# Recommender head on one core: inner rows in two stacked and two full tiles, gram copies split over SyncE and GpSimd, loads bound to other gathers

## The chip, the cores and the metric

The kernel runs on 1 core of one Trainium2 chip. The metric is the device time of one execution in microseconds (us). Three runs of the kernel before have a median of 208.22 us (207.81 to 209.19).

## The reference, cut to what matters

```python
sparse_embed = emb_tables[field_idx[None, :], x_sparse]        # 512 samples x 26 fields x 64, float32
z = sparse_embed.reshape(B, 26 * 64)                           # 1664 columns
gram = einsum('bik,bjk->bij', sparse_embed, sparse_embed)
inner = gram[:, iu, ju]                                        # 325 pairs i < j
dnn_in = concatenate([x_dense, z, inner], axis=-1)             # 13 + 1664 + 325 = 2002 columns
h = relu(dnn_in @ w1 + b1)                                     # w1 is 2002 x 2002
out = sigmoid(h @ w2 + b2)                                     # 512 x 1
```

## The kernel before, in words

**The product.** The 512 samples are four batch tiles of 128 (bt 0 to 3). The 2002 rows of w1 and the row of b1 lie in 16 tiles (K tiles t0 to t15) of up to 128 rows: t0 to t12 hold z (two tiles for a group of four fields, t12 alone for the last two fields), and t13 to t15, the inner tiles, hold the 325 pairs, the 13 dense columns and a row of ones for b1, with 117, 123 and 111 rows. The 2002 columns are cut into two halves (h 0, h 1) of two chunks of 500 or 502. A float32 product is made of three fp32r products: each operand is split into hi (its fp32r rounding, a cast on ScalarE) and lo (the rest, a subtraction on VectorE), and TensorE runs hi*hi, x_hi*w_lo and x_lo*w_hi. So one `product` (one w piece t, h with one bt) is 3 terms x 2 chunks = 6 matmuls of about 500 columns (L1071 to L1073 where it is the last of its sum, L1081, L1084 and L1087 elsewhere), and all of it is 16 x 2 x 4 = 128 products, 768 matmuls.

**The w pieces.** SyncE loads each piece of 500 KB into one of 5 buffers `w_raw` (L778), ScalarE casts it to `w_hi` (L849), VectorE makes `w_lo` in two halves (L931); there are 7 buffers for each of these. Phase A uses a piece for bt 0 and 1 (32 pieces), phases B1 (h 1) and B2 (h 0) for bt 2 and 3 (another 32). A load waits for the `w_lo` of the piece five before it, and up to load 26 also for a given number of gathers (`GATE`). The 1 MB of w2 goes behind load 28 (L781).

**The embeddings.** GpSimd issues 104 gathers (L823), each 128 rows of 256 bytes, four to one *arrival* (one bt, one group of four fields; two for the last group). Gathers 0 to 51 are for bt 0 and 1, gathers 52 to 103 for bt 2 and 3. From gather 52 on a short memset `pace` (L834) stands behind each. Gathers 56 and 60 are held until gram rounds 2 and 4 are done (`HELD_BACK`). VectorE transposes an arrival (L948, L944 for the last group), ScalarE casts it to `x_hi` (L875), VectorE makes `x_lo` (L961), and both copy it into `ET`, the layout of the gram matmuls.

**The gram rounds.** 64 small matmuls each (L1041): four rounds for bt 0 and 1, four for bt 2 and 3 together. Both engines copy the result from PSUM into `G` (L893, L979), and then DMAs put it into `x_in`, the rows of the inner tiles: pairs of a field below 13 with one of 13 or above go straight from G (*cross* pairs, L792, three DMAs for a bt), the pairs within one half of the fields go to `gram_dram` in HBM (*store*, L797, two DMAs) and from there skewed into `x_in` (*fetch*, L804, two DMAs of 84 rows, some of which carry pairs twice against rows of zeros in w). All seven are on SyncE's queue, in order with the w loads.

**The order.** `make_todo` writes TensorE's order by hand; `make_orders` plays the engines against each other with a table of durations (`PE_LEN`, `LAND` and so on), may pull a step of TensorE's forward where the next is not ready, and from that come the four lists that ScalarE, VectorE, TensorE and SyncE run strictly in order. GpSimd's order is the loop over the arrivals. TensorE starts with 25 matmuls on ones, and puts two more of 512 columns (`KEEP`, L1020) before its fourth product. Phase A ends with the inner tiles of bt 0 and 1, phase B with those of bt 2 and 3, after which only the last drains and the sigmoid are left.

## Time and profile before

| | us |
|---|---|
| median of 3 runs | 208.22 (207.81 to 209.19) |
| the profiled execution | 207.65 |
| its span | 205.1 |
| TensorE busy in it | 197.8 (96%) |
| VectorE, ScalarE, GpSimd busy | 146.6, 129.6, 118.5 |
| bytes moved | 38.99 MB, 190 GB/s on the mean |

The span is what the instructions cover; 2.55 us of the execution lie outside it. Times of rows are us from the start of the span. A busy time is what an engine spends in instructions; of a matmul the end is modelled, so that neighbouring rows overlap a little, and the distance from start to start is the better measure.

### The profile page before, as it was taken

The numbers are of one execution on the slowest core, as the hardware profiler recorded it, in microseconds if no ns is written. First come the engines' busy times: TensorE is split into PE (matmuls) and PEld (weight loads), VectorE is DVE, ScalarE is ACT, GpSimd is POOL, SyncE is SP. The second block draws the span as 40 slices with busy tenths as digits, with TensorE's granted clock in tenths as the row PEclk, the third lists the DMA queues.
The fourth block names the chain that finished last, engine by engine and source line by source line (L and its number), as shares of the span: only waits on it lengthen the run. The fifth ranks groups of instructions, "written<-read, shape, count | busy, mean of one in ns | idle before, by whom it ended". The sixth has DMA issues, their size and how long they took to land.

```text
span 205.1 us, 3837 instructions
## 1 busy us (share of the span) xinstructions
PE 197.8 (96%) x1334; PEld 160.8 (78%) x1334; DVE 146.6 (71%) x343; ACT 129.6 (63%) x260; POOL 118.5 (58%) x162
## 2 busy tenths in 40 slices
PE   8979999999999999989998999999999999999994
PEld 8946788888888778767885888888888887788882
DVE  3566877777885898679449999492978687563473
ACT  2766644778964999487528755676899946542201
POOL 4778778777777787369888988898920000000000
PEclk9999999999999999999999999999999999999998
DMA  5689767777776069837937748778598186023000
GB/s 153 179 254 312 234 220 225 216 231 207 225 231 250 20 208 316 297 71 209 370 124 224 209 140 268 276 249 298 132 327 280 13 283 210 6 48 59 28 0 0
DMA packets 15387, 38.99 MB, mean 190 GB/s; under 512 B 3881, under 2 KB 5281, under 8 KB 15369
## 3 DMA queue, kind: packets, MB, share of 16 engines
q1 hardware_dynamic: 11688, 35.27, 51.7%
q0 software_dynamic: 3328, 3.41, 8.6%
q8 instruction: 10, 0.16, 0.3%
q10 hardware_dynamic: 353, 0.08, 0.2%
q14 instruction: 8, 0.07, 0.1%
HBM read 37.71 MB, written 0.69 MB: 187 GB/s over the span
## 4 chain that ended last, share of the span: by engine, by line
PE 74%; DMA 8%; POOL 7%; DVE 4%; issue 3%; ACT 1%; DVEq 0%; ACTq 0%; POOLq 0%
PE slot L1081 23%; PE slot L1084 22%; PE slot L1087 22%; DMA E<-emb,row_idx 7%; POOL E L823 7%; PE slot L1041 3%; DVE slot L1005 1%; PE slot L1073 1%; PE slot L1071 1%; PE slot L1072 1%; DVE w_lo L931 1%; DMA x_idx<-idx 1%; PE slot L1020 1%; POOL pace L834 1%; DVE G L979 1%
## 5 line engine op out<-in xcount | busy, mean ns | idle before, releaser
L823 POOL DMA_INDIRECT E<-emb,row_idx x104 | 108.8, 1046 | 31.2 <-issue 23.7
L931 DVE TENSOR_TENSOR w_lo<-w_raw,w_hi 128x500 fp32r<-128x500 f32 (+6 forms) x128 | 80.6, 670 | 9.4 <-ACT w_hi L849 9.0
L849 ACT CAST w_hi<-w_raw 128x1000 fp32r<-128x1000 f32 (+6 forms) x64 | 65.0, 1028 | 22.7 <-DMA w_raw<-w 18.8
L1081 PE MATMUL slot<-w_hi,x_hi 128*128 128x500 f32 (+5 forms) x236 | 74.7, 397 | 1.4 <-ACT x_hi L867 1.0
L1084 PE MATMUL slot<-w_lo,x_hi 128*128 128x500 f32 (+5 forms) x236 | 73.4, 391 | 1.6 <-DVE w_lo L931 1.5
L1087 PE MATMUL slot<-w_hi,x_lo 128*128 128x500 f32 (+5 forms) x236 | 72.7, 389 | 0.0
L1084 PEld LDWEIGHTS slot<-w_lo,x_hi 128*128 128x128 f32 (+2 forms) x236 | 44.5, 188 | 11.8 <-DVE w_lo L931 2.7
L1081 PEld LDWEIGHTS slot<-w_hi,x_hi 128*128 128x128 f32 (+2 forms) x236 | 43.3, 189 | 12.5 <-ACT x_hi L875 1.7
L1087 PEld LDWEIGHTS slot<-w_hi,x_lo 128*128 128x128 f32 (+2 forms) x236 | 44.5, 189 | 9.1
L880 ACT COPY ET<-T 32x128 f32<-32x128 f32 (+4 forms) x86 | 31.1, 362 | 2.0
L948 DVE STREAM_TRANSPOSE T<-E 128x256 f32<-128x256 f32 x24 | 10.6, 441 | 19.3 <-DMA E<-emb,row_idx 19.2
L875 ACT CAST x_hi<-T 128x256 fp32r<-128x256 f32 x24 | 9.7, 406 | 14.5 <-DVE T L948 14.1
L966 DVE COPY ET<-T 32x128 f32<-32x128 f32 (+3 forms) x58 | 15.1, 261 | 1.8
L893 ACT COPY G<-slot 26x208 f32<-26x208 f32 x34 | 11.0, 324 | 7.5 <-PE slot L1041 6.7
L979 DVE COPY G<-slot 26x208 f32<-26x208 f32 x30 | 11.1, 370 | 4.2 <-PE slot L1041 3.4
L1005 DVE SCALAR_TENSOR_TENSOR slot<-slot,w_all 128x500 f32<-128x500 f32 (+1 forms) x16 | 10.7, 696 | 2.1 <-PE slot L1073 2.0
L1041 PEld LDWEIGHTS slot<-ET 64*64 64x64 f32 x512 | 8.7, 135 | 3.1 <-issue 2.4
L961 DVE TENSOR_TENSOR x_lo<-x_in,x_hi 117x128 fp32r<-117x128 f32 (+2 forms) x12 | 3.5, 292 | 10.5 <-ACT x_hi L867 10.5
L867 ACT CAST x_hi<-x_in 117x128 fp32r<-117x128 f32 (+2 forms) x12 | 3.6, 297 | 11.8 <-DMA x_in<-G 6.3
L961 DVE TENSOR_TENSOR x_lo<-T,x_hi 128x256 fp32r<-128x256 f32 x24 | 10.0, 418 | 1.3 <-ACT x_hi L875 1.2
L1041 PE MATMUL slot<-ET 64*64 64x52 f32 x512 | 9.7, 221 | 0.2 <-DVE G L979 0.2
L1013 PE MATMUL slot<-ones 128*128 128x128 f32 x50 | 8.3, 345 | 1.0 <-POOL ones L813 1.0
(39 smaller groups left out, 81.3 us busy)
## 6 DMA issues: line engine op xcount, KB each, us to landing
w_raw<-w SPq DMA_DIRECT2D x32, 501.0 KB, 4.7
w_raw<-w SPq DMA_DIRECT2D x32, 500.0 KB, 4.3
E<-emb,row_idx POOLq DMA_INDIRECT x104, 4.0
w_all<-w SPq DMA_DIRECT2D x1, 1001.0 KB
gram_dram<-G SPq DMA_DIRECT2D x8, 84.5 KB
x_in<-gram_dram SPq DMA_DIRECT2D x8, 42.0 KB
x_in<-G SPq DMA_DIRECT2D x4, 58.5 KB
x_in<-G SPq DMA_DIRECT2D x4, 19.5 KB
```

The lines of the kernel that those rows point to most:

```text
L823: nc.gpsimd.indirect_dma_start(out=E[:, k % ER, j, :], out_offset=None, in_=emb_rows, in_offset=bass.IndirectOffsetOnAxis(ap=row_idx[:, at ...
L849: nc.scalar.copy(w_parts(m)[0], w_source(m)).then_inc(w_hi_ready, 1)
L880: nc.scalar.copy(*et_copy(bt, part, i, h, half)).then_inc(et_by_act, 1)
L931: nc.vector.tensor_tensor(lo[:, cols], w_source(m)[:, cols], hi[:, cols].bitcast(F32), ALU.subtract)\
L961: nc.vector.tensor_tensor(lo, src, hi.bitcast(F32), ALU.subtract).then_inc(x_split, 1)
L966: nc.vector.tensor_copy(*et_copy(bt, part, i, h, half)).then_inc(et_by_dve, 1)
L979: nc.vector.tensor_copy(gram_place(bt % 2, s, rnd), gram_view(bt, s, b)).then_inc(g_copied_dve, 1)
L1005: nc.vector.scalar_tensor_tensor(out=acc, in0=acc, scalar=0.0, in1=w2_all[:, at:at + width], op0=ALU.max, op1=ALU.mult, accum_out=parts[:, ...
L1041: last = nc.tensor.matmul(slot[AUX[bt]][64 * c:64 * c + 64, at:at + 2 * FIELDS], e.rearrange("k s f -> k (s f)"), e[:, :, 0:FIELDS], start ...
L1081: nc.tensor.matmul(acc[q], xh, hi[:, cols[q]], start=first, stop=False)
L1084: nc.tensor.matmul(acc[q], xh, lo[:, cols[q]], start=False, stop=False)
L1087: last = nc.tensor.matmul(acc[q], xl, hi[:, cols[q]], start=False, stop=False)
```

## The change

**The inner rows.** They are now 339 rows (each pair once, dense, ones) in four tiles. 85 of them (`BOTH`: 78 cross pairs and 7 dense) are in the tiles TERMS_A (t13) and TERMS_B (t14), which hold the three terms as rows of one matmul: in TERMS_A rows 0 to 84 of `x_hi` meet `w_lo`, in TERMS_B rows 0 to 84 of `x_lo` (written into `x_hi` by VectorE) meet `w_hi`, and rows 85 and up of both carry hi*hi, 42 and 43 of them. The other 254 rows are in FULL_0 (t15) and FULL_1 (t16), with three matmuls a chunk as before. So a half of one bt takes 1 + 1 + 3 + 3 = 8 passes for its inner rows where it took 9. There are 68 w pieces for 64, and 4 casts of `x_in` a bt for 3.

**The copies.** SyncE makes four cross DMAs for a bt. GpSimd makes the two stores and now four fetches (36, 42, 42, 36 rows), at fixed places among the gathers (`BY_POOL`: the store of bt 0 before gather 58, its fetch before 60, the store of bt 1 before 61, its fetch before 63; those of bt 2 and 3 behind the last gather). SyncE no longer waits for a store.

**Loads and order.** Loads 2 to 9 and 26 wait for other gathers, w2 goes ahead of load 26 behind gather 47, `KEEP` is 1 for 2, the dense rows are loaded by SyncE in three DMAs. In phase B the B1 products of the last group (t10, t11) come after three groups of B2 instead of four, and the gram rounds of bt 2 and 3 stand among other B2 products.

```diff
-CROSS = [(0, 9), (9, 12), (12, 13)]
-IT = len(CROSS)
+IT = 4
 NT = ZT + IT
-CROSS_AT = [0, 0, DENSE]
-WITHIN_ROWS, WITHIN_COLS = HALF - 1, (HALF + 1) // 2
-WITHIN = WITHIN_ROWS * WITHIN_COLS
-WITHIN_AT = {1: 3 * HALF, 2: DENSE + HALF}
-ONES_AT = WITHIN_AT[2] + WITHIN
-KROWS = [P] * ZT + [9 * HALF, WITHIN_AT[1] + WITHIN, ONES_AT + 1]
+TERMS_A, TERMS_B, FULL_0, FULL_1 = range(ZT, NT)
+BOTH = 6 * HALF + 7
+CROSS_AT = [(TERMS_A, 0, 0, 6), (TERMS_A, BOTH + 3, 0, 3), (TERMS_B, BOTH + 4, 3, 6), (FULL_0, 0, 6, HALF)]
+SHORT = 6
+LONG = SHORT + 1
+WITHIN_AT = [(FULL_0, 7 * HALF, 0, SHORT, 2 * SHORT, SHORT), (FULL_1, 7, 0, 0, SHORT, LONG),
+             (FULL_1, 7 + SHORT * LONG, 1, 0, SHORT, LONG),
+             (FULL_1, 7 + 2 * SHORT * LONG, 1, SHORT, 2 * SHORT, SHORT)]
+KROWS = [P] * ZT + [BOTH + 3 + 3 * HALF, BOTH + 4 + 3 * HALF, 7 * HALF + SHORT * SHORT,
+                    7 + 2 * SHORT * LONG + SHORT * SHORT]
+DENSE_AT = [(TERMS_A, 6 * HALF, list(range(7)) + [0, 1, 2]), (TERMS_B, BOTH, [3, 4, 5, 6]),
+            (FULL_1, 1, [7, 8, 9, 10, 11, 12])]
+ONES_ROW = (FULL_1, 0)
 INNER_TILES = list(range(ZT, NT))
 IN_KEY = GROUPS_Z
+KEY_A, KEY_B = IN_KEY, IN_KEY + 1
+LO_AT = {t: n for n, t in enumerate(t for t in range(NT) if t not in (TERMS_A, TERMS_B))}
...
-GATE = {3: 4, 4: 5, 5: 7, 6: 8, 7: 9, 8: 11, 9: 12, 10: 15, 11: 16, 12: 19, 13: 20, 14: 23, 15: 24, 16: 27, 17: 28,
-        18: 31, 19: 32, 20: 35, 21: 36, 22: 39, 23: 40, 24: 41, 25: 43, 26: 51}
-CONSTS_BEHIND = 28
-KEEP_AT, KEEP = 3, 2
+GATE = {2: 3, 3: 3, 4: 6, 5: 7, 6: 8, 7: 11, 8: 12, 9: 13, 10: 15, 11: 16, 12: 19, 13: 20, 14: 23, 15: 24, 16: 27, 17: 28,
+        18: 31, 19: 32, 20: 35, 21: 36, 22: 39, 23: 40, 24: 41, 25: 43, 26: 50}
...
+CONSTS_AHEAD, CONSTS_GATE = 26, 47
+KEEP_AT, KEEP = 3, 1
...
+PACED_FROM = 3
 UNPACED = 52
+BY_POOL = {58: [("store", 0)], 60: [("fetch", 0)], 61: [("store", 1)], 63: [("fetch", 1)],
+           N_GATHERS: [("store", 2), ("store", 3), ("fetch", 2), ("fetch", 3)]}
...
         todo += b_group("B1", 1, g)
-        todo += b_group("B2", 0, GROUP_ORDER[n]) if n < 4 else []
-    rest = [s for g in GROUP_ORDER[4:] for s in b_group("B2", 0, g)]
-    todo += mixed(rest[:7], gram({2, 3}), every=2) + rest[7:]
+        todo += b_group("B2", 0, GROUP_ORDER[n]) if n < 3 else []
+    rest = [s for g in GROUP_ORDER[3:] for s in b_group("B2", 0, g)]
+    todo += rest[:1] + mixed(rest[1:9], gram({2, 3}), every=2) + rest[9:]
     later = [inner("B1", 1, 2), inner("B1", 1, 3), inner("B2", 0, 2), inner("B2", 0, 3)]
-    todo += [s for steps in later for s in steps[:1]] + [s for steps in later for s in steps[1:]]
+    todo += [s for steps in later for s in steps[:2]] + [s for steps in later for s in steps[2:]]
...
+def shelf(pieces, m):
+
+    return m - sum(PIECES[n][1] == TERMS_B for n in pieces[:m + 1])
+
+
+def earlier(pieces, m):
+
+    return [n for k, n in enumerate(pieces[:m]) if shelf(pieces, k) == shelf(pieces, m) - HL]
...
+        def cross_moves(bt):
+
+            rows = Q * (bt % 2)
+            return [(t - ZT, x_in[at:at + HALF * (b - a), bt, t - ZT, :], G[rows + a:rows + b, HALF:FIELDS, :])
+                    for t, at, a, b in CROSS_AT]
+
+        def within_store(bt, u):
+
+            within, rows = slice(HALF * u, HALF * (u + 1)), Q * (bt % 2) + HALF * u
+            return gram_dram[bt, u].rearrange("(i j) b -> i j b", i=HALF), G[rows:rows + HALF, within, :]
+
+        def within_fetches(bt):
+
+            skewed = [gram_dram[bt, u, 0:2 * SHORT * (HALF + 1), :].rearrange("(a e) b -> a e b", e=HALF + 1) for u in (0, 1)]
+            return [(t - ZT, x_in[at:at + (b - a) * far, bt, t - ZT, :], skewed[u][a:b, 1:far + 1, :])
+                    for t, at, u, a, b, far in WITHIN_AT]
...
-                    if m == EARLY:
-                        sp.wait_ge(e_landed[0], 16 * GROUP_GATHERS[LAST])
+                    if m == CONSTS_AHEAD:
+                        sp.wait_ge(paced, paced_count(CONSTS_GATE))
+                        sp.dma_start(w2_all[:], w2.rearrange("n o -> (o n)").partition_broadcast(P))\
+                          .then_inc(consts_landed, 16)
+                        sp.dma_start(b2_all[:], b2.partition_broadcast(P)).then_inc(consts_landed, 16)
                     if m in GATE:
-                        sp.wait_ge(paced, GATE[m] - SOON + 1)
-                    if m >= RAW:
-                        sp.wait_ge(w_split, 2 * (m - RAW + 1))
+                        sp.wait_ge(paced, paced_count(GATE[m]))
+                    if m >= RAW and PIECES[USED[m - RAW]][1] == TERMS_B:
+                        sp.wait_ge(w_hi_ready, w_hi_count(m - RAW))
+                    elif m >= RAW:
+                        sp.wait_ge(w_split, w_split_count(m - RAW, 1))
 
                     sp.dma_start(w_raw[:, m % RAW, 0:HALF_W[h]], w1[t, :, HALF_AT[h]:HALF_AT[h] + HALF_W[h]])\
                       .then_inc(w_landed[m % RAW], 16)
...
-                if op == ("load", CONSTS_BEHIND):
-                    sp.dma_start(w2_all[:], w2.rearrange("n o -> (o n)").partition_broadcast(P))\
-                      .then_inc(consts_landed, 16)
-                    sp.dma_start(b2_all[:], b2.partition_broadcast(P)).then_inc(consts_landed, 16)
-                if op[0] == "store":
+                if op == ("load", EARLY + 1):
+                    sp.wait_ge(pads_ready, 2)
...
+                        at += len(cols)
+                if op[0] == "cross":
                     bt = op[1]
-                    rows = Q * (bt % 2)
                     sp.wait_ge(g_copied_act, evac_count("act", rounds_of(bt)))
                     sp.wait_ge(g_copied_dve, evac_count("dve", rounds_of(bt)))
-                    if bt == 0:
...
+                    for m, to, src in cross_moves(bt):
+                        sp.dma_start(to, src).then_inc(cross_landed[bt][m], 16)
...
+            def move(part, bt):
+                if part == "store":
+                    pool.wait_ge(g_copied_act, evac_count("act", rounds_of(bt)))
+                    pool.wait_ge(g_copied_dve, evac_count("dve", rounds_of(bt)))
+                    for u in (0, 1):
+                        pool.dma_start(*within_store(bt, u)).then_inc(g_stored[bt], 16)
+                if part == "fetch":
+                    pool.wait_ge(g_stored[bt], 32)
+                    for m, to, src in within_fetches(bt):
+                        pool.dma_start(to, src).then_inc(within_landed[bt][m], 16)
+
...
             at = 0
             for k, (bt, g) in enumerate(ARRIVALS):
+                for part in BY_POOL.get(at, []):
+                    move(*part)
...
                 for j in range(GROUP_GATHERS[g]):
+                    for part in BY_POOL.get(at, []) if j else []:
+                        move(*part)
                     nc.gpsimd.indirect_dma_start(
...
+                    if g == KEY_B:
+                        dve.wait_ge(x_hi_ready, x_hi_count(bt, KEY_A))
+                        b = slice(bt * P, (bt + 1) * P)
+                        nc.vector.tensor_tensor(x_hi[0:BOTH, TERMS_B, b], x_in[0:BOTH, bt, TERMS_A - ZT, :],
+                                                x_hi[0:BOTH, TERMS_A, b].bitcast(F32), ALU.subtract).then_inc(x_split, 1)
+                    else:
...
+                    if t in (TERMS_A, TERMS_B):
+
+                        if t == TERMS_A:
+                            pe.wait_ge(x_hi_ready, x_hi_count(*key_of(step)))
+                        else:
+                            pe.wait_ge(x_split, x_lo_count(*key_of(step)))
+                            pe.wait_ge(w_hi_ready, w_hi_count(RANK[n]))
+                        for q in (0, 1):
+                            if t == TERMS_A:
+                                pe.wait_ge(w_split, w_split_count(RANK[n], q))
+                            last = nc.tensor.matmul(acc[q], xh, hi[:, cols[q]], start=first, stop=end)
+                            if end and q == 0:
+                                last.then_inc(half_done, 1)
```

What this moves is seen at two places. The first is where bt 0's gram is copied out, at the end of phase A. On SyncE's queue before (`x_in<-G` is a cross DMA, `gram_dram<-G` a store, `x_in<-gram_dram` a fetch, `w_raw` a load; the two bt follow each other):

```order
L778 DMA w_raw<-w 128x1000 x2
L792 DMA x_in<-G 117x1x128
L797 DMA gram_dram<-G 13x1664 x2
L792 DMA x_in<-G 39x1x128
L792 DMA x_in<-G 13x1x128
L804 DMA x_in<-gram_dram 84x1x128 x2
L778 DMA w_raw<-w 128x1000
```

SyncE's queue now, at the same place:

```order
L861 DMA w_raw<-w 128x1000
L875 DMA x_in<-G 78x1x128
L875 DMA x_in<-G 39x1x128 x2
L875 DMA x_in<-G 91x1x128
L861 DMA w_raw<-w 128x1000 x3
```

And GpSimd's now, where before only `DMA E` and `MEMSET pace` alternate; the first `DMA E` here is gather 57, the one behind the first fetches is gather 60:

```order
L908 DMA E<-emb,row_idx 128x64
L919 MEMSET pace 128x64
L891 DMA gram_dram<-G 13x1664 x2
L908 DMA E<-emb,row_idx 128x64
L919 MEMSET pace 128x64
L908 DMA E<-emb,row_idx 128x64
L919 MEMSET pace 128x64
L895 DMA x_in<-gram_dram 36x1x128
L895 DMA x_in<-gram_dram 42x1x128 x2
L895 DMA x_in<-gram_dram 36x1x128
L908 DMA E<-emb,row_idx 128x64
L919 MEMSET pace 128x64
```

Twelve DMAs (these six and the same six for bt 1) are now issued between gathers 57 and 63, and each gather from 58 on stands behind some or all of them.

The second place is TensorE's last product of bt 1's z and the first inner products of bt 0 (slot1 is the sum of bt 1, slot0 that of bt 0). Before, from the last rows of t11 over t13 to the first of the next product:

```order
L1087 MATMUL slot1<-w_hi,x_lo 128x500
L1081 MATMUL slot0<-w_hi,x_hi 128x502
L1081 MATMUL slot0<-w_hi,x_hi 128x500
L1084 MATMUL slot0<-w_lo,x_hi 128x502
L1084 MATMUL slot0<-w_lo,x_hi 128x500
L1087 MATMUL slot0<-w_hi,x_lo 128x502
L1087 MATMUL slot0<-w_hi,x_lo 128x500
L1081 MATMUL slot0<-w_hi,x_hi 128x502
```

Now, with TERMS_A and TERMS_B (L1176, two matmuls each; the lo buffer of a shared shelf holds the w of TERMS_B), and then FULL_0:

```order
L1202 MATMUL slot1<-w_hi,x_lo 128x500
L1176 MATMUL slot0<-w_hi,x_hi 128x502
L1176 MATMUL slot0<-w_hi,x_hi 128x500
L1176 MATMUL slot0<-w_lo,x_hi 128x502
L1176 MATMUL slot0<-w_lo,x_hi 128x500
L1196 MATMUL slot0<-w_hi,x_hi 128x502
L1196 MATMUL slot0<-w_hi,x_hi 128x500
L1199 MATMUL slot0<-w_lo,x_hi 128x502
```

The first tile that needs a fetch (t14 before, FULL_0 now) comes after 4 matmuls instead of 6.

## Rows read from the trace of the kernel before

**Rows 1.** The page: span, busy times, and TensorE's granted clock in 40 slices.
```profile
span 205.1 us, 3837 instructions
PE 197.8 (96%) x1334; PEld 160.8 (78%) x1334; DVE 146.6 (71%) x343; ACT 129.6 (63%) x260; POOL 118.5 (58%) x162
...
PEclk9999999999999999999999999999999999999998
```

**Rows 2.** Waits of TensorE: waited for, us in total, times, longest.
```profile
PE slot L1084 <- DVE w_lo L931: 1.5, 2, 1.0
...
PE slot L1081 <- ACT x_hi L867: 1.0, 1, 1.0
```

**Rows 3.** Timeline of TensorE, phase B: start, us, instruction, xcount, [idle before].
```profile
160.93 0.62 PE L1081 MATMUL slot<-w_hi,x_hi 128*128 128x500 f32 x2
...
162.29 0.61 PE L1081 MATMUL slot<-w_hi,x_hi 128*128 128x500 f32 x2
...
166.48 1.18 PE L1041 MATMUL slot<-ET 64*64 64x52 f32 x64
...
201.69 0.39 PE L1073 MATMUL slot<-w_hi,x_lo 111*128 111x500 f32 x1
```

**Rows 4.** Timeline of all engines, the start of phase A.
```profile
7.29 0.95 POOL L823 DMA_INDIRECT E<-emb,row_idx  x1 [0.30 <-issue]
11.34 0.31 DVE L944 STREAM_TRANSPOSE T<-E 128x128 f32<-128x128 f32 x1 [1.39 <-DMA E<-emb,row_idx]
```

**Rows 5.** Timeline where bt 1's fourth group arrives, at the end of phase A.
```profile
71.14 0.41 ACT L875 CAST x_hi<-T 128x256 fp32r<-128x256 f32 x1
71.60 0.71 PE L1081 MATMUL slot<-w_hi,x_hi 128*128 128x500 f32 x2
```

**Rows 6.** Timeline of SyncE and GpSimd around the copies of bt 0 and 1.
```profile
80.47 0.95 POOL L823 DMA_INDIRECT E<-emb,row_idx  x1 [0.16 <-issue]
...
81.08 1.00 SPq L792 DMA_DIRECT2D x_in<-G  x1
...
82.13 1.01 SPq L797 DMA_DIRECT2D gram_dram<-G  x2
...
87.51 2.43 SPq L804 DMA_DIRECT2D x_in<-gram_dram  x2
...
88.83 0.95 POOL L823 DMA_INDIRECT E<-emb,row_idx  x1 [4.68 <-DVE T L948]
...
90.64 0.84 SPq L792 DMA_DIRECT2D x_in<-G  x1
91.53 1.25 SPq L797 DMA_DIRECT2D gram_dram<-G  x2
...
92.91 1.29 POOL L823 DMA_INDIRECT E<-emb,row_idx  x1 [0.16 <-issue]
...
95.63 1.62 SPq L804 DMA_DIRECT2D x_in<-gram_dram  x2
```

**Rows 7.** Gathers: by form over the span, the last, its arrival, and landings from 94 to 151.
```profile
L823 POOL DMA_INDIRECT E<-emb,row_idx x104 | 108.8, 1046 | 31.2 <-issue 23.7 <-DVE T L948 4.8 <-DVE row_idx L918 1.8
...
148.92 1.18 POOL L823 DMA_INDIRECT E<-emb,row_idx  x1 [0.16 <-issue]
...
153.67 0.45 DVE L948 STREAM_TRANSPOSE T<-E 128x256 f32<-128x256 f32 x1 [0.58 <-DMA E<-emb,row_idx]
...
E<-emb,row_idx POOLq DMA_INDIRECT x41, 3.7
```

**Rows 8.** SyncE: stores and fetches by tile: count: ns min/median/max, first to last.
```profile
L797 SPq DMA_DIRECT2D gram_dram<-G x8: 453/505/693, 82.1 to 185.7; - x8
L804 SPq DMA_DIRECT2D x_in<-gram_dram x8: 756/786/1597, 87.5 to 190.5; - x8
```

**Rows 9.** Waits on the fetched rows in the last stage of phase B.
```profile
188.00 3.22 SPq L804 DMA_DIRECT2D x_in<-gram_dram  x4
190.31 0.30 ACT L867 CAST x_hi<-x_in 123x128 fp32r<-123x128 f32 x1 [2.35 <-DMA x_in<-gram_dram]
```

214 lines of the change are left out of this document (118 added, 96 removed).

## The prediction

> **What bounds the kernel now.** I read the page first: TensorE is busy 197.8 of 205.1 us [rows 1], so time is won by giving it less, or lost by making it wait. Then its waits: 2.5 us in three places in all of phases A and B [rows 2]. Next the timeline of TensorE, for the price of a step: the product that starts at 160.93 ends where the next starts, at 162.29, so 6 matmuls take 1.37 us, one 0.228; the gram round at 166.48 lasts 1.18 and costs some 1.3 with the restart behind it [rows 3]. The last matmul starts at 201.69 and ends at 202.1; the 3.0 us from there to the end of the span are drains, sigmoid and the store, which the change leaves as they are. The profiled execution took 207.65, 0.57 under the median of 208.22, so the sum is made on 202.1 for TensorE's end and its difference is put on the median.
>
> Last I looked for who comes just in time. GpSimd does: its gathers go out back to back until 148.92, and the arrival that ends with that one is turned at 153.67 [rows 7]. TensorE takes it at 160.93 [rows 3].
>
> **What is removed.** Eight passes for nine over the inner rows, 2 chunks, 4 bt, 2 halves: 16 matmuls x 0.228 = 3.65 us less, all of it on TensorE, which waits for little. Four more w pieces cost ScalarE 4 casts, VectorE nothing (TERMS_B has no lo) and the queues 2 MB on 39; with ScalarE busy 129.6 of 205.1 and VectorE's count unchanged [rows 1] they have cover.
>
> **The start.** The fourth gather goes out at 7.29 and its arrival is turned at 11.34 [rows 4], 4.0 us later; load 2 is issued behind the first arrival, in the midst of that. It now waits for this gather, and a filler matmul pair is gone. Up to 1.5 us could be won here. But bt 1's fourth group reaches x_hi at 71.14 + 0.41 = 71.55, and TensorE takes it at 71.60 [rows 5]: 45 us later phase A is at the pace of the gathers, which are not sooner. Whoever is early there waits there. Bounds 0 and 1.5; I take 0.3, near the row that binds.
>
> **The copies of bt 0 and 1, and what stands behind them.** SyncE gets free: its fetch at 87.51 had waited for the store of 82.13 [rows 6] with the loads behind. GpSimd takes that wait. Before, it had a hole from 84.0 to 88.83, held by the gram rounds [rows 6]; that hides a part. Its clock now, with s for a store DMA and f for a fetch DMA: gather 57 at 80.47, next free at 81.75; bt 0's gram has been copied by 81.08, so the two stores go at once. Gathers 58 and 59 take 2 x 1.28. The stores land 4.4 us after they are issued (83.14 to 87.51 [rows 6]), then four fetches. Gather 60 not before 88.83. Store of bt 1 not before 90.6, gathers 61 and 62, landing at most 2.9 (92.78 to 95.63), four fetches, gather 63, which went at 92.91.
>
> The trace has no plain DMA issued by GpSimd, so s and f are bounded from both sides. Below: SyncE's shortest of these, 0.45 [rows 8]. Above: a gather on GpSimd itself, 1.05 on the mean and 1.28 from start to start [rows 6, 7]. I take SyncE's medians for the same shapes, with the gap that GpSimd shows: s 0.55 and f 0.80 (0.50 and 0.79 [rows 8]), since 13 or 40 rows are less to write than a gather's 128. Then: stores to 82.85, gathers to 85.4, landing 87.25, fetches to 90.45, gather 60 to 91.7, stores to 92.8, gathers to 95.4, landing 95.7, fetches to 98.9. Gather 63 is D = 6.0 us late, and so is each of the 40 behind it, as GpSimd has no idle time later in which to catch up. At 0.45 each D is 3.2, at 1.25 it is 12.4.
>
> Against this, DMAs from GpSimd have a rule of their own. The gathers here last 1.05 on the mean against 0.95 for most single ones [rows 6, 7], though VectorE copies ET from SBUF to SBUF between them. The Trainium skill (SBUF — State Buffer, "Who interferes with whom") says that a VectorE copy in its two-port mode shuts GpSimd out, descriptor writing with it, and gives 620 ns alone against 3100 beside such a copy. The trace does not show a gather three times as long, so that end is not used; 0.62 for each of the twelve would, as an estimate from that page, give D of 5.
>
> **What the late gathers cost.** The order now asks sooner: from the product that takes the last arrival (B1, t10, bt 3) to TensorE's end there are 24 full products, 8 short ones of 2 matmuls and 4 gram rounds, 24 x 1.37 + 8 x 0.456 + 4 x 1.33 = 41.8 us, and before there were 26 products and 4 rounds, 40.9 (202.1 - 160.93 is 41.2). The last gather goes at 148.92 + D, lands 3.7 (median of 41) to 4.75 later (its own, 153.67 - 148.92) [rows 7], and transpose 0.45, cast 0.41 and two hand-overs make 0.95 [rows 5, 7]. So TensorE can't end before 148.92 + 4.2 + 0.95 + 41.8 + D = 195.9 + D. With no wait for gathers it would end at 202.1 - 3.65 - 0.3 = 198.15. The first is the later one as soon as D is over 2.3. With D = 6.0 it is 201.9: 0.2 under the 202.1 of before. The 3.95 us won are given back to within 0.2 in waits for x_hi in B1.
>
> **Waits that this covers.** FULL_0 of bt 0 is wanted some 1.0 earlier than t14 was (4 matmuls for 6 ahead of it, and the start), and its fetch is issued at 88.05 against 87.51, FULL_1's last by 90.45. With a landing of 2.3 (188.00 to 190.31 [rows 9]) to 3.3, x_hi is there at 91 to 93 and TensorE waits 1 to 2 us where it waited 1.0 [rows 2], and about 1 again at bt 1. These waits come before the B arrivals, so below some 3.5 in sum they only shorten those. At the end the fetches of bt 3 are issued by some 11 us behind the last copy from PSUM and land at 13.5; FULL_1 of bt 3 is wanted 17.3 behind the last gram round (7 products, 8 short ones, 3 full ones), of which the copies take some 2: nothing. VectorE runs its list in order, and transposes late by D hold the w_lo behind them; I count 0.1 for it, bounds 0 and 1.5.
>
> **Sum.** 207.65 - 0.2 + 0.1 = 207.55, and on the median's scale 208.1.
>
> **Rivals.** *GpSimd's plain DMAs cost nearly what its gathers do (slower).* The place is gathers 58 to 63. For it: GpSimd writes descriptors for a plain copy too, and a good part of a gather's 0.95 [rows 6] may be fixed. Against: a tenth to a third of the rows. At 1.0 each D is 9.4 and TensorE ends at 205.3, the time is 211.4; at 1.25 D is 12.4 and the time 214.4. It decides from D = 8.2, some 0.87 each, where 1% is lost. If waits for x_hi grow to several us the granted clock, full until the last slice before [rows 1], could also drop; no row prices that.
>
> *They are cheap, or arrivals land sooner (faster).* With TensorE waiting, loads thin out, and half of the landings are under 3.7 as it is [rows 7]. At 0.5 each D is 3.5; with a landing of 3.7 the end is 198.9, the time 205.0; nothing under 198.15 less a full start, 196.9. For it: SyncE's rows, and its queue no longer blocks loads. Typical of it is 205.2.
>
> *The start pays in full and carries.* Gathers 56 and on hang on gram rounds, so D moves with TensorE; if the arrivals of phase A land sooner for loads 4 to 9 standing behind other gathers, 1.2 more is won, 206.9. It stays within 1%, and is part of the forecast's case.
>
> *The stacking doesn't shorten anything.* The short matmuls have 127 and 128 rows and the same 500 columns; rows of 111, 117 and 128 rows all take 0.228. Not likely, and it would add 3.65 only if gathers didn't bind.
>
> **How the numbers follow.** Forecast (D of 4.5 to 8, waits in B1 for most of what was won): 0.37, 206.4 to 210.3. Dear DMAs: 0.31. Cheap ones: 0.32. The measurement tells about 1% from no change, so faster by over 1% has 0.32, within 1% 0.37, slower by over 1% 0.31. The range for 8 in 10 leaves a tenth at either side: 204.5 (D near 3.2, part of the start) to 213.3 (1.15 each).
>
> **What would show it.** Right: 752 matmuls of 500 columns, GpSimd's DMA rows at 0.55 to 0.8, gather 63 at 98 to 100 and the last at 154 to 156, and 3 to 5 us of TensorE's waits on x_hi L962 between 110 and 160, the longest at t10. Wrong: gather 63 before 96 with TensorE's end under 200, or after 101; waits in B on w_lo and not on x_hi; more than 4 us of waits at t15 and t16 in phase A; or a granted clock under full in B.

## The result: slower by 1.7%, and the profile after

The changed kernel took 212.43 us (211.73 to 212.49, 4 runs) beside 208.7 us for the kernel before (207.81 to 209.95, 4 runs), a ratio of 1.0166 with a 95% interval of 1.0105 to 1.0228. The profiled execution took 211.73 us with a span of 209.8, before 207.65 with 205.1 [rows 1]. The forecast was no change (208.1): the time lies inside the range, on the slower side. The medians here and below are of all runs, and the ratios leave out the few that fell in a slower state of the chip, the profiled one of i1 among them.

From the page of the changed kernel: span, busy times, TensorE's granted clock in 40 slices, the chain by engine.

```profile
span 209.8 us, 3872 instructions
...
PE 198.1 (94%) x1316; PEld 160.6 (77%) x1316; DVE 147.3 (70%) x345; ACT 135.0 (64%) x267; POOL 133.3 (64%) x186
...
PEclk9997899999999999997999999999996999999999
...
PE 50%; POOL 24%; DMA 12%; issue 5%; DVE 3%; SPq 3%; ACT 2%; ACTq 0%; DVEq 0%; POOLq 0%
```

TensorE has 16 matmuls and a filler less and is busy for as long as before, because the clock row, full before, has three dents. GpSimd holds 24% of the chain that ended last, where its share had been 7%; before, the row was:

```profile
PE 74%; DMA 8%; POOL 7%; DVE 4%; issue 3%; ACT 1%; DVEq 0%; ACTq 0%; POOLq 0%
```

The DMAs that I could only bound are cheap. GpSimd's stores and fetches by tile (ns min/median/max, first to last start), against SyncE's in [rows 8]:

```profile
L895 POOL DMA_DIRECT2D x_in<-gram_dram x16: 569/608/646, 87.9 to 194.3; - x16
L891 POOL DMA_DIRECT2D gram_dram<-G x8: 518/552/572, 83.2 to 185.8; - x8
```

Now TensorE's waits, with the clock behind each. The timeline of TensorE in the changed kernel (start, us, instruction, [idle before <- releaser]):

```profile
18.23 0.79 PE L1196 MATMUL slot<-w_hi,x_hi 128*128 128x500 f32 x2 [1.79 <-ACT x_hi L962]
...
95.93 0.49 PE L1185 MATMUL slot<-w_hi,x_hi 127*128 127x502 f32 x1 [1.78 <-DVE x_lo L1061]
...
107.37 0.50 PE L1185 MATMUL slot<-w_hi,x_hi 127*128 127x502 f32 x1 [1.43 <-DVE x_lo L1061]
...
157.40 0.72 PE L1196 MATMUL slot<-w_hi,x_hi 128*128 128x500 f32 x2 [1.98 <-ACT x_hi L962]
...
164.52 0.61 PE L1196 MATMUL slot<-w_hi,x_hi 128*128 128x500 f32 x2
...
206.41 0.39 PE L1187 MATMUL slot<-w_hi,x_lo 127*128 127x500 f32 x1
```

And its windows (stretch, length, TensorE busy, granted clock, DMA share, GB/s):

```profile
17.00:18.85 1.85, 0.62 (x3) 0.97 0.87 312
18.85:22.10 3.25, 3.25 (x9) 0.50 0.77 232
22.10:24.00 1.90, 1.90 (x10) 0.99 0.85 251
...
97.20:100.60 3.40, 3.40 (x10) 0.50 0.77 235
...
158.60:161.90 3.30, 3.30 (x9) 0.51 0.04 10
```

Three of the four waits are followed by 3.3 us at half clock, the 1.2 GHz level. A matmul takes 0.415 us there (159.01 to 159.43 in the timeline) for 0.228, so a stretch loses some 1.5 us. GpSimd's timeline around the stores and fetches of bt 0 and 1, against [rows 6]:

```profile
80.87 0.95 POOL L908 DMA_INDIRECT E<-emb,row_idx  x1 [2.75 <-PE slot L1142]
...
83.19 1.12 POOL L891 DMA_DIRECT2D gram_dram<-G  x2
...
87.92 2.39 POOL L895 DMA_DIRECT2D x_in<-gram_dram  x4 [0.79 <-DMA gram_dram<-G]
90.65 1.12 POOL L908 DMA_INDIRECT E<-emb,row_idx  x1 [0.34 <-issue]
...
93.03 1.08 POOL L891 DMA_DIRECT2D gram_dram<-G  x2 [1.09 <-DVE G L1080]
...
97.73 2.39 POOL L895 DMA_DIRECT2D x_in<-gram_dram  x4 [0.79 <-DMA gram_dram<-G]
100.42 1.02 POOL L908 DMA_INDIRECT E<-emb,row_idx  x1 [0.30 <-issue]
...
157.52 1.11 POOL L908 DMA_INDIRECT E<-emb,row_idx  x1
```

Gather 63 goes at 100.42 for 92.91, the last one at 157.52 for 148.92. VectorE's timeline says what a late gather does in phase A:

```profile
103.08 0.36 DVE L1061 TENSOR_TENSOR x_lo<-x_in,x_hi 127x128 fp32r<-127x128 f32 x1
106.50 0.45 DVE L1042 STREAM_TRANSPOSE T<-E 128x256 f32<-128x256 f32 x1 [3.05 <-DMA E<-emb,row_idx]
...
107.04 0.28 DVE L1061 TENSOR_TENSOR x_lo<-x_in,x_hi 127x128 fp32r<-127x128 f32 x1
```

The transpose is that of arrival 17, which ends with gather 63. VectorE is held there for 3.05 us, and behind it in the list stands x_lo of FULL_1 of bt 1, for which TensorE waits at 107.37.

TensorE's wait at 157.40 is for the last arrival but one, that of bt 2, and not for the last one. In phase B, VectorE, then ScalarE:

```profile
156.47 0.45 DVE L1042 STREAM_TRANSPOSE T<-E 128x256 f32<-128x256 f32 x1 [2.02 <-DMA E<-emb,row_idx]
160.16 0.45 DVE L1042 STREAM_TRANSPOSE T<-E 128x256 f32<-128x256 f32 x1
...
162.42 0.40 ACT L962 CAST x_hi<-T 128x256 fp32r<-128x256 f32 x1
```

The first transpose is that of bt 2's arrival, whose last gather went at 151.40, 5.1 us earlier; TensorE takes it at 157.40. The last arrival (bt 3) is cast by 162.82, and TensorE, which does the two products of bt 2's arrival and two of B2 first, takes it only at 164.52.

**Where 4.7 us went, by stage.** Times of TensorE in each profiled execution: start of the first gram round, end of the last one of phase A, start of phase B, end of the last matmul; then GpSimd's last gather, and how far TensorE ends behind it. The start of phase B is marked at the third matmul of the product behind the last inner one, some 0.46 us into it; in f3, f5, j1, k2, l1, m2 and m3 one product of phase B (1.37 us) has already been done at that mark. All kernels stand here, as the experiments are read from the same columns (ratios and medians are with each). Each row is one execution.

| kernel | first gram | gram A ends | B starts | end | last gather | end less gather |
|---|---|---|---|---|---|---|
| before | 73.15 | 88.03 | 107.89 | 202.08 | 148.92 | 53.2 |
| changed | 74.46 | 89.80 | 112.04 | 206.80 | 157.52 | 49.3 |
| e1_keep3 | 74.33 | 90.59 | 114.71 | 206.39 | 158.09 | 48.3 |
| e2_sync | 73.97 | 91.08 | 116.53 | 209.99 | 151.90 | 58.1 |
| e3_order_b | 73.77 | 90.33 | 115.69 | 209.19 | 159.39 | 49.8 |
| e4_before_pool | 74.22 | 89.23 | 112.23 | 206.51 | 155.83 | 50.7 |
| g2_chain_cut | 78.83 | 93.88 | 117.97 | 209.96 | 161.13 | 48.8 |
| g1_chain_cut_no_dma | 77.73 | 92.79 | 111.83 | 203.30 | 154.38 | 48.9 |
| f2_inner_land | 73.01 | 89.04 | 115.72 | 206.79 | 157.14 | 49.7 |
| f3_both_land | 73.10 | 89.13 | 115.50 | 206.27 | 156.53 | 49.7 |
| i1_swap | 74.53 | 93.21 | 114.32 | 210.39 | 159.78 | 50.6 |
| f4_told | 72.95 | 89.07 | 110.64 | 207.39 | 155.91 | 51.5 |
| f5_told_order | 73.02 | 88.81 | 111.31 | 205.05 | 156.65 | 48.4 |
| j1_stores_sync | 73.00 | 89.26 | 111.83 | 206.67 | 158.00 | 48.7 |
| k2_fetch65 | 73.57 | 90.11 | 112.35 | 206.07 | 155.66 | 50.4 |
| k5_fetch65_old | 73.49 | 89.59 | 112.97 | 207.13 | 154.37 | 52.8 |
| l1_act_fetch | 73.10 | 90.12 | 113.76 | 204.67 | 151.71 | 53.0 |
| m1_w2_late | 73.40 | 88.49 | 112.07 | 205.94 | 156.54 | 49.4 |
| m2_w2_act | 74.08 | 89.34 | 113.09 | 204.49 | 153.83 | 50.7 |
| m3_w2_31 | 73.03 | 88.17 | 114.90 | 206.02 | 148.39 | 57.6 |

Changed less before: 1.3 us by the first gram round (this execution has the wait at 16.4 and the half clock behind it), 0.5 in the gram stage, 2.4 from there to phase B, 0.6 in phase B. The stacking takes 8 matmuls, 1.8 us, out of each of the last two, so these lose 4.2 and 2.4; 1.3 + 0.5 + 4.2 + 2.4 - 3.65 = 4.7. Of the 4.2, 2.4 are waits (3.4 in three places between 92 and 108, before 0.97 in one) and 1.5 the clock.

### The profile page after: what moved, and what is told of

It is laid out like the page before. It is cut to its first block, busy times and chain, and to the rows that moved or that the text cites. A ratio compares the mean times of both kernels' runs of the same rounds, so it can differ in the third digit from the quotient of the medians.

```text
span 209.8 us, 3872 instructions
## 1 busy us (share of the span) xinstructions
PE 198.1 (94%) x1316; PEld 160.6 (77%) x1316; DVE 147.3 (70%) x345; ACT 135.0 (64%) x267; POOL 133.3 (64%) x186
## 4 chain that ended last, share of the span: by engine, by line
PE 50%; POOL 24%; DMA 12%; issue 5%; DVE 3%; SPq 3%; ACT 2%; ACTq 0%; DVEq 0%; POOLq 0%
POOL E L908 20%; PE slot L1196 14%; PE slot L1199 13%; PE slot L1202 13%; DMA E<-emb,row_idx 8%; PE slot L1142 4%; SPq L875 3%; POOL pace L919 2%; DMA gram_dram<-G 2%; PE slot L1176 2%; DMA x_in<-G 1%; DVE G L1080 1%; PE slot L1187 1%; PE slot L1185 1%; PE slot L1186 1%
## 5 line engine op out<-in xcount | busy, mean ns | idle before, releaser
L1025 DVE TENSOR_TENSOR w_lo<-w_raw,w_hi 128x500 fp32r<-128x500 f32 (+3 forms) x120 | 75.7, 671 | 12.6 <-ACT w_hi L936 12.3
L936 ACT CAST w_hi<-w_raw 128x1000 fp32r<-128x1000 f32 (+3 forms) x64 | 65.2, 1029 | 22.3 <-DMA w_raw<-w 11.0
L1196 PE MATMUL slot<-w_hi,x_hi 128*128 128x500 f32 (+3 forms) x220 | 70.8, 403 | 4.2 <-ACT x_hi L962 3.8
L1199 PE MATMUL slot<-w_lo,x_hi 128*128 128x500 f32 (+3 forms) x220 | 69.3, 396 | 0.1
L1202 PE MATMUL slot<-w_hi,x_lo 128*128 128x500 f32 (+3 forms) x220 | 68.3, 392 | 0.0
L1196 PEld LDWEIGHTS slot<-w_hi,x_hi 128*128 128x128 f32 (+1 forms) x220 | 41.3, 192 | 14.7 <-ACT x_hi L962 5.4
L1199 PEld LDWEIGHTS slot<-w_lo,x_hi 128*128 128x128 f32 (+1 forms) x220 | 42.3, 192 | 9.5 <-DVE w_lo L1025 0.8
L1202 PEld LDWEIGHTS slot<-w_hi,x_lo 128*128 128x128 f32 (+1 forms) x220 | 42.0, 191 | 8.8
L895 POOL DMA_DIRECT2D x_in<-gram_dram x16 | 9.4, 607 | 5.6 <-DMA gram_dram<-G 4.2
L1185 PE MATMUL slot<-w_hi,x_hi 127*128 127x500 f32 (+2 forms) x20 | 8.5, 423 | 3.2 <-DVE x_lo L1061 3.2
```

Of the source, the lines that this page charges most:

```text
L936: nc.scalar.copy(w_parts(m)[0], w_source(m)).then_inc(w_hi_ready, 1)
L1025: nc.vector.tensor_tensor(lo[:, cols], w_source(m)[:, cols], hi[:, cols].bitcast(F32), ALU.subtract)\
L1196: nc.tensor.matmul(acc[q], xh, hi[:, cols[q]], start=first, stop=False)
L1199: nc.tensor.matmul(acc[q], xh, lo[:, cols[q]], start=False, stop=False)
L1202: last = nc.tensor.matmul(acc[q], xl, hi[:, cols[q]], start=False, stop=False)
```

## The experiments

Four theories came up in turn. A: each wait of some 2 us costs as much again by the clock. B: the late gathers bind phase B. C: the fetched rows come late to the inner stage of phase A. D: VectorE's in-order list passes the gathers' lateness on to the inner stage.

**e1_keep3.** `KEEP_AT, KEEP = 3, 1` became `3, 3`.

> Only the filler before the fourth product changes: 3 matmuls of 512 columns for 1, so that TensorE is busy through the 1.8 us in which it waited at 16.4 us. Theory A (a wait of about 2 us is followed by some 3.4 us at a granted clock of 0.50, and that costs another 1.6 us): the clock stays at full at 19 to 22 us, gram round 2 ends some 1.6 us sooner, gathers 56 and on too, and the time is 1.0 to 1.8 us less than that of the changed kernel, 210.6 to 211.4. Theory B (only the late gathers count, the start is levelled out at the pace of the gathers): within 0.5 us of the changed kernel's 212.4.

211.65 us, ratio 1.0132 (1.0051 to 1.0213). The clock stays full at 19 to 22 and the wait shrinks to 0.39, yet the first gram round begins at 74.33: no sooner than the changed kernel's 74.46. The time is in neither theory's range, and the interval overlaps that of the changed kernel; theory A gets nothing certain.

**e2_sync.** SyncE issues the stores behind its first direct copy, and the fetches:

```diff
-BY_POOL = {58: [("store", 0)], 60: [("fetch", 0)], 61: [("store", 1)], 63: [("fetch", 1)],
-           N_GATHERS: [("store", 2), ("store", 3), ("fetch", 2), ("fetch", 3)]}
+BY_POOL = {N_GATHERS: []}
...
                 sp_events.append((at, ("cross", bt)))
+                sp_events.append((at + 4.0, ("fetch", bt)))
```

> The changed kernel with its 8 stores and 16 fetches issued by SyncE, the fetches four entries behind the copies, every other order as it is. Theory B (GpSimd's own DMAs and the waits in front of them, which hold the gathers back by 7.5 to 8.6 us, are the loss): gather 63 is back at 93 to 95, the last one at 150 to 152, no wait at the product of t10 of bt 2, and the time is 3.5 to 5 us less, 207.5 to 209. Theory A: the waits at 16.4 and at FULL_1 of bt 0 and the slow clock behind them stay, only the third wait with its slow stretch goes: 3 to 3.6 us less, about 209. A rival to both (SyncE, held by its waits for the stores, now issues w loads late): waits on w_hi or w_lo at 90 to 110, and less than 1.5 us won.

213.44 us, 1.0188 (1.0110 to 1.0266): both theories miss, and the rival is borne out. The last gather is at 151.90 as expected and the wait at t10 is gone, and nothing is won. SyncE, which has six more DMAs per bt, issues bt 1's fetches at 101.09 instead of 97.73, and the next w piece only behind them, at 104.14. ScalarE stands 3.27 us at the cast of a w piece, with FULL_1's cast behind it in its list, and TensorE waits 3.2 us for what comes of that. SyncE, ScalarE, TensorE:

```profile
101.09 3.00 SPq L883 DMA_DIRECT2D x_in<-gram_dram  x4
...
108.72 1.02 ACT L944 CAST w_hi<-w_raw 128x1000 fp32r<-128x1000 f32 x1 [3.27 <-DMA w_raw<-w]
...
110.32 0.49 PE L1193 MATMUL slot<-w_hi,x_hi 127*128 127x502 f32 x1 [3.18 <-DVE x_lo L1069]
```

**e3_order_b.** Phase B's order as before:

```diff
-        todo += b_group("B2", 0, GROUP_ORDER[n]) if n < 3 else []
-    rest = [s for g in GROUP_ORDER[3:] for s in b_group("B2", 0, g)]
-    todo += rest[:1] + mixed(rest[1:9], gram({2, 3}), every=2) + rest[9:]
+        todo += b_group("B2", 0, GROUP_ORDER[n]) if n < 4 else []
+    rest = [s for g in GROUP_ORDER[4:] for s in b_group("B2", 0, g)]
+    todo += mixed(rest[:7], gram({2, 3}), every=2) + rest[7:]
```

> The changed kernel with the order of phase B as before (B2 of the fourth group too stands ahead of B1's last group), so that the arrivals of t10 and t11 are asked for some 5 us later. Theory A: the wait of 2.0 us at 155.4 and the 1.5 us of slow clock behind it go, 2.5 to 3.5 us less, 209 to 210. Theory B in its strict form (TensorE can't end before the last gather plus the work that stands behind it): 4 products move ahead of the last arrival, so there is as much to win, the two agree here and differ only in the clock row of 157 to 162. If something else holds phase B, nothing is won.

213.51 us, 1.0188 (1.0107 to 1.0269): both theories miss, and nothing is won, as in the last case. The wait at t10 is gone, but phase B starts at 115.69 in an order that is the changed kernel's up to there (which had 112.04), and at the end TensorE waits 0.7 for a gram copy and 1.6 for rows copied straight from G. So the end of phase A can lie 3 to 4 us apart in two profiled executions with the same lists up to there, and a difference of that size in one row of the table shows nothing by itself.

**e4_before_pool.** The kernel before, with its stores and fetches issued by GpSimd ahead of gathers 58, 60, 61, 63 (the changed kernel's `BY_POOL` and `move`, on the shapes of before).

> The kernel before with one part of the change alone: its 8 stores and 8 fetches on GpSimd at the places where the changed kernel has them, all orders of the other engines as before. The gathers behind become 12 DMAs less 4 late: some 5 us at 0.55 to 0.61 each, with the waits for the stores perhaps 6. The last arrival, turned at 153.67 before and asked for at 160.93, is then ready at 159 to 160. Theory A: no wait over 1 us comes in phase B and the clock stays full, the time is within 1 us of before. Theory B: the order before has the slack, so the same, but every us over 7 of lateness costs one. If the lateness is paid in phase A (FULL fetched rows, in-order transposes), 1 to 3 us slower.

211.79 us, 1.0124 (1.0074 to 1.0173): slower than before by itself, which takes the last of the three cases. No stacking, no new start and no slow clock are in it, and it loses 4.3 us by the start of phase B (1.1 of them by the first gram round, ahead of all that was moved). From its timelines, GpSimd, TensorE and VectorE:

```profile
89.44 1.29 POOL L820 DMA_DIRECT2D x_in<-gram_dram  x2 [2.86 <-DMA gram_dram<-G]
...
93.93 0.72 PE L1101 MATMUL slot<-w_hi,x_hi 123*128 123x502 f32 x2 [1.76 <-ACT x_hi L883]
...
106.41 0.45 DVE L966 STREAM_TRANSPOSE T<-E 128x256 f32<-128x256 f32 x1 [6.56 <-DMA E<-emb,row_idx]
...
107.09 0.72 PE L1107 MATMUL slot<-w_hi,x_lo 123*128 123x502 f32 x2 [1.45 <-DVE x_lo L979]
```

GpSimd stands 2.86 us at the landing of the stores, the fetches go 1.9 later than SyncE's [rows 6], and at bt 1 the transpose of arrival 17 stands ahead of x_lo again.

**g2_chain_cut and g1_chain_cut_no_dma.** FULL_0 and FULL_1 of bt 0 and 1 are made from rows put in place at the start, and don't wait for copies or fetches. So in both, those inner rows are not the gram's; in g1 the stores and fetches of bt 0 and 1 are also left out.

```diff
+                    for t, row in ((FULL_0, 0), (FULL_1, 7)):
+                        sp.dma_start(x_in[row:127, 2:4, t - ZT, :], w1[t, row:127, 0:2 * P]...)
...
-                        for landed, count in arrivals_of(bt, m):
+                        for landed, count in arrivals_of(bt, m) if bt >= 2 or m < 2 else []:
...
+            from_bt = bt + 2 if bt < 2 and m >= 2 else bt
```

> The changed kernel, in which the two tiles FULL_0 and FULL_1 of bt 0 and bt 1 are made from rows that a DMA put in place at the start, and no longer wait for the copies and fetches (so these inner rows are not those of the gram; all stores, copies and fetches are still issued where they were, and the gathers are as late). Theory C (what costs is the wait of the inner stage of phase A for its fetched rows, 3.4 to 5.2 us between 88 and 112 in the four kernels that have the rows fetched late, and what the clock loses behind it): no wait over 0.5 us there, phase B starts at 107.5 to 109 instead of 112 to 115.7; then the late gathers (last one at 156 to 158) bind, TensorE ends no sooner than 157 + 4.2 + 0.95 + 41.8 = 204, and the time is 209.5 to 210.5. Theory B (the gathers alone count): the same time. Theory A (waits wherever they are, with a slow clock behind each): the wait at t10 grows by what is won here, 3 to 5 us in B, and the time stays at 211 to 212.5.

> As the kernel with the chain cut, and the stores and fetches of bt 0 and 1 are left out altogether, so that GpSimd's gathers are on time (gather 63 at 92 to 94, the last one at 149 to 151). Neither the wait for fetched rows nor the late gathers are left: what remains against before is the stacking, 3.65 us less, and the start. Theories B and C alike: 204 to 206 us. If it is over 207, something that is neither of the two costs as much as the stacking wins, and the casts and copies on ScalarE and VectorE or the start are next. The difference to the kernel with the chain cut alone is the price of the 12 DMAs on GpSimd with fetched rows out of the way: 4 to 5 us by theory B, below 2 if the gathers had slack.

g2: 215.83 us, 1.0331 (1.0255 to 1.0408). g1: 208.28 us, 0.9986 (0.9944 to 1.0028). The rows put in place are two DMAs on SyncE ahead of a w piece: both kernels wait some 3 us for w_hi at 21 to 24 (2.7 and 3.0), and g1's first gram round is 3.3 us behind the changed kernel's, g2's 4.4. So the times aren't to be read by themselves, but the stages are. From the first gram round to the end, before takes 128.9 us, the changed kernel 132.3, g2 131.1 and g1 125.6. With neither in the way the changed kernel wins 3.4 us, near the stacking's 3.65, though before had a wait of 0.97 for fetched rows in that stretch that g1 has not; with the 12 DMAs of bt 0 and 1 put back on GpSimd (the only edit between the two) all of it is gone, though no inner tile waits for a fetched row. The medians differ by 7.5 us the same way, where the first gram rounds lie 1.1 apart. g2's forecast of no wait over 0.5 us is missed (2.4 and 1.45 are left), g1's of 204 to 206 by about its late start. That speaks for theory D: in g2 VectorE still stands at the transpose of arrival 17 with x_lo behind it, and TensorE with it. VectorE, then TensorE:

```profile
110.90 0.45 DVE L1046 STREAM_TRANSPOSE T<-E 128x256 f32<-128x256 f32 x1 [2.50 <-DMA E<-emb,row_idx]
...
111.78 0.68 PE L1189 MATMUL slot<-w_hi,x_hi 127*128 127x502 f32 x1 [2.40 <-DVE x_lo L1065]
```

**f2_inner_land and f3_both_land.** The planner's landing times, in f3 also the order of phase A's end:

```diff
-INNER_LAND = (3.9, 4.7, 9.2, 10.4)
+INNER_LAND = (3.9, 4.7, 11.0, 12.5)
...
-    todo += inner_0[2:] + later[0] + [s for steps in later[1:] for s in steps[:2]]
-    todo += [s for steps in later[1:] for s in steps[2:]]
+    todo += later[0][:2] + inner_0[2:] + later[0][2:] + [s for steps in later[1:] for s in steps[:2]]
+    todo += [product("B1", ZT - 1, 1, 2)] + [s for steps in later[1:] for s in steps[2:]]
```

> The changed kernel with the planner told that FULL_0 and FULL_1 come 11.0 and 12.5 us behind the last copy (it assumed 9.2 and 10.4; the trace shows 12.7 from the copies' DMA to the cast of FULL_1 of bt 1). ScalarE and VectorE then do other work ahead of those casts, so that less stands blocked behind them, and TensorE takes the short products first. If in-order blocking (a turn, a w_lo or a cast standing behind one that waits for fetched rows) is a good part of the loss: 0.5 to 1.5 us less than the changed kernel. If the fetched rows themselves are late, within 0.5 us of it.

> The changed kernel with the same numbers for the planner and another order of phase A's end: the short products of both halves ahead of FULL_0 and FULL_1 of bt 0 (0.9 us more for their rows), and the first product of phase B (t12 of bt 2, whose row tile has long arrived) ahead of the FULL products of bt 1, with all short ones (1.4 to 1.8 us more). Theory C: the waits of the inner stage shrink from 3.4 to 5.2 us to 1 to 2.5, phase B's rest starts 2 us sooner, the time is 1 to 2.5 us less than the changed kernel's, 210 to 211.4. Theory B: nothing is won, since the late gathers bind at t10: 212 to 212.5.

f2: 211.79 us, 1.0159 (1.0089 to 1.0230); f3: 213.21 us, 1.0252 (1.0192 to 1.0312). f2 is 0.6 us under the changed kernel with an interval that overlaps its own, f3 missed both ranges. The waits of the inner stage were 6.3 and 5.5 us. In f3 the transpose of arrival 17 waits 5.27 us. Both kernels end 49.7 us behind the last gather, as the changed one does (49.3).

**i1_swap.** One entry of VectorE's list:

```diff
+DVE_OPS.remove(("turn", 17))
+DVE_OPS.insert(DVE_OPS.index(("x_lo", 1, IN_KEY + IT - 1)) + 1, ("turn", 17))
```

> The changed kernel with one entry of VectorE's list moved: the transpose of arrival 17, whose last gather is gather 63 (behind all stores and fetches of bt 0 and 1), stands behind the two subtractions for x_lo of bt 1's last inner tiles instead of ahead of the last one. Theory D (the wait in phase A at 107 to 111 us is that of VectorE, which is held at this transpose for 3 to 5 us with x_lo of FULL_1 behind it): TensorE's wait on x_lo at 107 to 111 (1.4, 2.3, 1.4, 3.2 us in the four kernels with this order) is under 0.6, the time is 1 to 2.5 us less than the changed kernel, 210 to 211.4. Theory C (the fetched rows themselves are late): the wait stays, now on x_hi, within 0.5 us of 212.4. If what is won is paid at t10 in phase B for the late gathers (theory B), the wait moves there and the time stays.

213.11 us, 1.0174 (1.0092 to 1.0256). The wait on x_lo at 109.65 is 0.58, as theory D said; the wait at t10 is 2.69 in place of 1.98, as the last sentence said. D is right about the wait and wrong about the time. The profiled execution is the slowest of the four, 215.17 us, and had lost 3.3 us more than the changed kernel's in the gram stage, ahead of this place, so its wait is worth more here than its stage times.

**f4_told, f5_told_order, j1_stores_sync.** The planner is told what GpSimd's DMAs take (f5: with f3's edits, j1: and the stores on SyncE behind its first copy):

```diff
+MOVES_TAKE = {58: 1.1, 60: 2.9, 61: 1.2, 63: 2.8}
...
                 n = len(g_issued)
+                pool_at += MOVES_TAKE.get(n, 0.0)
```

> The changed kernel with the planner told how long GpSimd is held by its stores and fetches (1.1, 2.9, 1.2 and 2.8 us ahead of gathers 58, 60, 61 and 63; it counted them at nothing), so that it places all transposes, and what hangs on them, by gathers that are 8 us late. The transpose of arrival 17 then stands 10 entries behind x_lo of FULL_1, and t10's products of phase B come 3 products later. Theory D with theory B (late gathers cost only where a list expects them on time): neither the wait at 107 nor the one at 157, the time is 3 to 4.5 us less than the changed kernel, 208 to 209.4. Theory C: the inner stage's waits for fetched rows stay at 2 to 3 us, 210 to 211.

> As the kernel with the planner told of GpSimd's DMAs, and also told that fetched rows come at 11.0 and 12.5 us, with the short products first and t12 of bt 2 ahead of the FULL products of bt 1. Theory D: the last waits of the inner stage go too, 0.5 to 1.5 us less than with the planner told alone, 207 to 208.5. If the order of phase A's end brought nothing in the kernel with that order because it has other costs (a drain, a w piece more in the buffers), it is no faster than with the planner told alone.

> As the one before, with the 8 stores issued by SyncE behind the first of its direct copies (the fetches stay on GpSimd): GpSimd is freed of 4 store DMAs at 0.55 and of its wait for the last copies (1.1 us), so gather 63 goes 2.5 to 3.5 us sooner, at 97 to 98, and the last one at 153.5 to 155. Theory B: another 1 to 3 us less where the late gathers bind, 205.5 to 207.5. If the gathers are no longer what binds: within 0.7 us of the kernel before this one.

212.10 us, 1.0157 (1.0079 to 1.0234); 212.04, 1.0184 (1.0110 to 1.0259); 211.25, 1.0102 (1.0038 to 1.0166). All three forecasts of a gain are missed; f5 is no faster than f4, as its second case had it. Told, the planner has phase B start at 110.64 for 112.04, and TensorE still ends at 207.39, 51.5 behind the last gather: it waits 1.5 us for x_hi at 152.75 and 1.8 for gram copies at 170.91, where two gram rounds now stand one behind the other. In j1 GpSimd has 4 DMAs less before gather 63 and sends it no sooner, at 101.27, for it stands at its fetches until SyncE's stores have landed:

```profile
88.22 2.37 POOL L899 DMA_DIRECT2D x_in<-gram_dram  x4 [4.16 <-DMA gram_dram<-G]
...
98.63 2.34 POOL L899 DMA_DIRECT2D x_in<-gram_dram  x4 [3.50 <-DMA gram_dram<-G]
```

**k2_fetch65, k5_fetch65_old, l1_act_fetch.** Stores on SyncE ahead of its copies; fetches where the stores have landed (k5 without the new order of phase A's end; the names behind # say which kernel has the line):

```diff
+BY_POOL = {60: [("fetch", 0)], 65: [("fetch", 1)], N_GATHERS: [("fetch", 2), ("fetch", 3)]}   # k2, k5
+BY_POOL = {60: [("fetch", 0)], N_GATHERS: [("fetch", 2), ("fetch", 3)]}                       # l1
...
+                        if (bt, g) == (1, KEY_A):                                             # l1, ScalarE
+                            act.wait_ge(g_stored[bt], 32)
+                            for n, to, src in within_fetches(bt):
+                                act.dma_start(to, src).then_inc(within_landed[bt][n], 16)
```

> The stores go out on SyncE ahead of its direct copies, the fetches on GpSimd ahead of gathers 60 and 65 (not 63), where the stores have landed; the planner is told (2.2 and 2.8 us), and has the order with the short products first. GpSimd then has 8 DMAs at 0.6 in its way instead of 12 and waits for no landing: gather 63 at 94.5 to 97, the last one at 153 to 155. Gathers bind (TensorE ends 48 to 50 us behind the last gather): TensorE's end at 201.5 to 204.5, time 207 to 210. The chain binds (fetched rows as late as in the changed kernel): phase B starts at 110 to 112, and 94 us of phase B less 1.8 put the end at 203 to 205, 208.5 to 210.5. If both are relieved for good: under 207.

> The same places for stores and fetches, with the order of phase A's end as in the changed kernel. If the order with the short products first brings what it was made for, this one has 1 to 2 us more of waits for fetched rows and is 1 us slower than the one before; if it costs as much as it brings, the same.

> As the first of the three, with the four fetches of bt 1 issued by ScalarE, behind its cast of the first terms' rows of bt 1 (about 98 us), so that in phase A only the four fetches of bt 0 stand between GpSimd's gathers, most of them in the hole before gather 60. Gather 63 at 93 to 95, the last one at 150 to 152; gathers bind nowhere. If the gathers' lateness was the main loss: 205 to 207.5. If the chain is: fetched rows of bt 1 reach x_lo at 104 to 106 as before and the time is within 1 us of the kernel with the fetches at 65. ScalarE pays 4 DMAs, some 2 us, beside its 135 us of work.

212.32 us, 1.0237 (1.0017 to 1.0456); 211.41, 1.0124 (0.9868 to 1.0380); 210.08, 1.0129 (1.0001 to 1.0256). The runs of before are spread wide in this set (206.47 to 210.90), so only the medians order them, and weakly. k2's ranges are missed, k5 is not slower than k2, and l1 is 2.2 us faster than k2. In l1 the last gather is at 151.71 and TensorE ends 53.0 behind it, so the gathers no longer bind; but phase B starts at 113.76, as ScalarE takes 3.52 us for the four fetches (0.88 each) and TensorE waits 1.47 for the terms whose cast stands behind them.

**m1_w2_late, m2_w2_act, m3_w2_31.** w2 goes out behind load 28 as before, load 26 behind gather 51 (m1: in the changed kernel; m2: in l1; m3: m2 with w2 behind load 31):

```diff
-        18: 31, 19: 32, 20: 35, 21: 36, 22: 39, 23: 40, 24: 41, 25: 43, 26: 50}
+        18: 31, 19: 32, 20: 35, 21: 36, 22: 39, 23: 40, 24: 41, 25: 43, 26: 51}
-CONSTS_AHEAD, CONSTS_GATE = 26, 47
+CONSTS_BEHIND = 28
```

> The changed kernel with w2, b2 and the gate of load 26 as before: w2 behind load 28 (about 74 us) instead of behind gather 47 (67.4), load 26 behind gather 51. If the early traffic is what makes arrival 13 and with it gram rounds 2 and 3 late: the stretch 70 to 75 moves under 100 GB/s, the transpose of arrival 13 starts at 76.5 to 77 and waits under 0.5, the last gram round of phase A ends 1 to 1.5 us sooner against the first, and the time is 0.5 to 1.5 us less than the changed kernel's 212.4, since gathers 56 and on hang on the gram rounds. If not: within 0.5 us.

> The fastest version so far (210.1: stores on SyncE ahead of its copies, bt 0's fetches on GpSimd, bt 1's on ScalarE, planner told, short products first) with w2 and load 26 as before. Gathers do not bind in it (TensorE ends 53 us behind the last one), so what the gram rounds win comes through whole: 1 to 2 us less, 208 to 209, the same as before within what can be measured. A rival: w2 now meets the loads and copies of 75 to 90 us, and bt 0's fetched rows or the direct copies come later by what was won.

> The version with w2 behind load 28 (209.3), with w2 behind load 31 (about 88 to 90 us, where the stretch 85 to 90 moves little). If w2 in the stretch 75 to 85 delays the landing of bt 0's stores: these land 3.5 us after they are issued instead of 5 to 6, GpSimd's first fetch goes out at 87 instead of 89.5, TensorE's two waits for FULL_0 and FULL_1 of bt 0 (0.95 and 1.92) shrink to under 1.5 in sum, and the time is 0.7 to 1.5 us less, 207.8 to 208.6. If w2 now meets bt 1's moves and w pieces at 90 to 95: the same time, with the waits moved to 103 to 108.

m1: 210.85 us, 1.0102 (1.0036 to 1.0169). m2: 209.26 us, 1.0037 (0.9997 to 1.0076). m3: 211.88 us, 1.0157 (1.0118 to 1.0195). m1's time and traffic are as expected, the step between them is not. The transpose of arrival 13 starts at 76.50 where the changed kernel has 77.63, but in both it waits for no gather and stands 3.1 to 3.2 us behind the start of the first gram round, which m1 reaches 1.1 us sooner; the last gram round ends 15.1 us behind that start where it was 15.3, not 1 to 1.5 us less. The effect of w2 shows in the other kernels. In the twelve that have w2 at 67 to 70 us and the start's loads as the changed kernel (e1 to e3, f2 to l1) the transpose waits 1.1 to 3.1 us for its gathers and this stage takes 15.8 to 18.7 us; in the five with w2 behind load 28 or later (before, e4, m1, m2, m3) it waits for none and takes 14.9 to 15.3. l1 and m2, with this edit alone between them, have 2.5 us and none, 17.0 and 15.3. In the changed kernel's own profiled execution TensorE came to the first gram round late and the gathers were there (so too in g1 and g2). From e1, where they were not:

```profile
78.68 0.45 DVE L1042 STREAM_TRANSPOSE T<-E 128x256 f32<-128x256 f32 x1 [1.12 <-DMA E<-emb,row_idx]
```

Windows of the changed kernel, then of m1 (stretch, length, clock, DMA share, GB/s):

```profile
70.00:75.00 5.00, 1.00 0.77 256
```

```profile
70.00:75.00 5.00, 1.00 0.27 46
75.00:80.00 5.00, 1.00 0.95 278
80.00:85.00 5.00, 1.00 1.01 372
```

The price is there too: with 80 to 85 full, GpSimd waits 2.76 us for bt 0's stores (0.79 in the changed kernel) and TensorE 2.24 for the rows. m2 is the version to set beside the changed kernel: its interval lies wholly under that one's, and does not reach as far as 1% over before. m3 is a miss that teaches: bt 0's stores do land sooner (its fetches go at 85.71 for 89.49), but w2 and four w pieces go out together at 87 to 91, one of these keeps ScalarE waiting for 3.8 us with the cast of FULL_1 behind it, as in e2, and TensorE waits 3.7 us:

```profile
87.50 0.43 SPq L860 DMA_DIRECT2D w_all<-w  x1
...
96.98 1.02 ACT L938 CAST w_hi<-w_raw 127x1000 fp32r<-127x1000 f32 x1 [3.82 <-DMA w_raw<-w]
...
98.58 0.79 PE L1191 MATMUL slot<-w_hi,x_hi 127*128 127x502 f32 x1 [3.74 <-DVE x_lo L1067]
```

## Why the prediction was wrong

**The stacking's 3.65 us: right.** 16 matmuls at 0.228 are gone, and g1 is 3.4 us faster than before from the first gram round on where neither fetched rows nor GpSimd's DMAs are in the way.

**s and f: s right, f high.** 0.55 and 0.61 for 0.55 and 0.80; the rival of dear DMAs is refuted, although D passed the 8.2 that it named. (The Trainium skill, SBUF — State Buffer, "A bandwidth-pool intuition that's wrong (but worth ruling out)", has some 620 ns for a GpSimd DMA alone and some 3100 beside a VectorE copy; the longest of the 24 took 0.646, so the first agrees and the second shows nowhere here.) From gather 57 to 63 before took 12.44 us and the changed kernel takes 18.27: 5.8 of lateness, where the step said 6.0. That it is so near is in part luck: with 0.61 for a fetch the step's own sum gives 4.5, and the rest is what it left out, above all 1.1 us in which GpSimd stands at bt 1's stores for the last copy out of PSUM.

**D as a whole: the step that failed.** D is 8.6, not 6.0. I took gather 57 to go at 80.47, as before, and GpSimd not to fall further behind after gather 63. It went at 82.15, 1.7 later, since gather 56 hangs on gram round 2 and TensorE had come to the first of them 1.3 us late; 5.8 came between gathers 57 and 63, and 1.1 more over the last 40 gathers. By the prediction's own formula that alone moves TensorE's end from 201.9 to 204.5; it came at 206.8. That D moves with TensorE stood in the rival of the good start, for the winning side alone.

**The work behind the last gather: 47.0 foreseen, 49.3 measured.** This is the second term that was too small, by 2.3. The formula follows the last arrival, and the one that held TensorE was the arrival before it: gather at 151.40, TensorE at 157.40, so 6.0 for landing and hand-overs where the formula has 5.15, then four products more than it counts. The half clock behind that wait, 1.5 us, was put at nothing; the text said that no row prices it. From the last arrival's product at 164.52 to the end it is 42.3 us, for 41.8 foreseen. (Against the formula: 6.1 less for the earlier gather, 0.9 more for its landing, 5.5 for four products, 1.6 for the clock, 0.5 for the rest.) How far such a bound holds in general is open: of the 14 kernels that issue bt 1's stores or fetches on GpSimd ahead of the last gathers, 12 end 48.3 to 50.7 us behind the last gather, and the other two are f4 (51.5) and k5 (52.8, with a late start of phase B and 2.0 us for gram copies). But e1, e4 and f2 wait in phase B for no arrival by more than 0.3 us and end no nearer to it, and g1, without those DMAs, ends 48.9 behind: gathers 56 and 60 hang on gram rounds, so the last gather moves with TensorE itself.

**Waits that this covers: wrong by its logic.** I had the inner stage's waits at 2 to 3 us, "before the B arrivals", and let the gathers' bound swallow them. Their size was nearly right (3.4 with the one behind VectorE's list), by luck: the fetched rows of bt 0 and 1 landed 5.2 us (median) behind their issue, not 2.3 to 3.3, and TensorE came to them 1.3 us later than before. The half clock was not in it, and they aren't swallowed. There are two bounds that lie close together. Phase B alone takes 91.1 to 91.7 us from its start where it hardly waits (f2, e1), so the changed kernel, starting it at 112.04, could not end before 203.4, and by the gathers not before 204.5 by my own formula at its D. Before stood at 202.1. Either bound alone is a loss. That fits i1, where only the wait behind the transpose was taken away, and l1, where the gathers no longer bind and phase B still starts late; e2 doesn't test it, as its w pieces came late. e4 shows that moving the stores and fetches to GpSimd is enough for 1.2% by itself.

**The transposes behind which x_lo stands.** "I count 0.1 for it, bounds 0 and 1.5" was a step on w_lo in phase B. The place was x_lo in phase A, at arrival 17: 1.4 us here, 2.4 in g2. The upper bound was the right number.

**w2 and the later gates: not priced.** The prediction costs the start's loads and leaves w2's new place, 1 MB at 67.4 instead of 74.2, without a word. Undoing it took the median from 212.43 to 210.85; the intervals overlap, so its size, about 1.5 us, is less sure than its way, which the waits of arrival 13's transpose and the length of the gram stage show over these kernels.

**The start: 0.3 of gain foreseen, 1.3 of loss by the first gram round in the profiled execution.** The loss is not shown to be the change's. Seven kernels with the same start (f2, f3, f4, f5, j1, l1, m3) reach the round at 72.95 to 73.1, as before does, which is the argument from the gathers' pace. But m2 and i1, with that start and at full clock from 19 to 22 too, reach it at 74.08 and 74.53, and e4, with the start of before, at 74.22. So one start spreads by as much as the 1.3.

**The signs.** Right were GpSimd's DMA rows; gather 63 at 100.42 and the last one at 157.52 lie behind their ranges of 98 to 100 and 154 to 156, and of the 3 to 5 us of waits on x_hi between 110 and 160 there were 1.98, at t10. One sign of being wrong came: a granted clock under full in B.

What stays open: how much each of these is worth in the median, since single edits move it by about the width of the interval, and the two bounds hide each other. What is shown is that the moved stores and fetches cost time by themselves (e4, and g2 against g1), and the sum of what m2 undoes, by m2 against the changed kernel. No version beats before: the chain of bt 0 and 1 (copies, store, landing, fetch, landing) takes 15.4 us from the last gram round to the cast of FULL_1 in the changed kernel and 12.6 to the last cast of bt 1's rows before, and in no version that has it whole was it under 15.4.

## What to carry to other kernels

An instruction given to an engine whose work is paced (here one gather after another) costs its own time once, but its wait too, and all that is behind it moves; count from where that engine really stands, and ask in both directions what moves with it. Where a gain makes two other limits bind within a microsecond of each other, undoing either may show nothing: measure each stage from marks in the trace, and take both away at once. A list that an in-order engine follows is only as good as the times it was planned with: after moving DMAs, look for the entry that now waits and at what stands behind it (a transpose that waits for a gather, or a cast that waits for a w piece, as in e2 and m3), and give big one-off transfers a place of their own in the table of what is moved.

## What the runs showed of the hardware that I had not expected

TensorE's granted clock went to 0.50 for about 3.3 us behind waits of 1.8 to 2 us, but not each time. At the same place, the wait near 17 us, the changed kernel fell after 1.79 us and j1 stayed at full clock after 1.81, k2 after 2.24. Windows of j1 (columns as above):

```profile
17.00:19.00 2.00, 0.69 (x3) 1.00 0.92 353
19.00:21.00 2.00, 2.00 (x11) 1.00 0.58 118
```

So such a fall can be priced (1.5 us) and not foreseen from one wait's length. And it isn't the whole loss: k2, l1, j1 and m2 show full clock in their profiled executions and are not faster than before.

The fetches of 36 or 42 rows of 512 bytes for bt 0 and 1 land 5.2 us after GpSimd issues them in the changed kernel (median by form in the DMA view), longer than its gathers' 4.1 from 94 to 151; in k2 it is 2.4 and 3.5, in f3 6.0 and 6.8, so it is no fixed price. Issued by ScalarE they take it 0.88 us each (l1), by GpSimd 0.61 (2.39 for four), while SyncE issues a store in 0.37 when its stores go first (0.73 for two, k2) and in 0.55 to 0.65 between copies (e2, j1).
